# Routing tails, the openings of two phases and where expert weights are fetched, in a two-layer kernel on one core

## The reference

```python
x = x + L0_attn(ln(x))   # a state-space scan: W_in, W_A, W_B, W_C, W_out, rms norm
x = x + L0_ffn(ln(x))    # 8 experts, 2 per token: relu(x @ w1 + b1) @ w2 + b2
x = x + L1_attn(ln(x))   # 16 heads of 16, causal, rotary positions
x = x + L1_ffn(ln(x))    # 16 experts, 2 per token, and a shared expert:
#   shared = silu(x @ Sg) * (x @ Su) @ Sd
#   probs = softmax(x @ Wr); top 2 experts e with weight p:
#   routed = sum of p * (silu(x @ Wg[e]) * (x @ Wu[e]) @ Wd[e])
```

## Time and profile before

| | |
|---|---|
| median of 3 runs | 1963.16 us (1962.06 to 1966.38) |
| the profiled execution | 1963.09 us |
| its span, first to last instruction | 1961.4 us |
| busy TensorE / VectorE / ScalarE / GpSimd | 1638.4 / 1024.0 / 699.0 / 565.0 us |
| instructions | 29495 |

### The profile page before, as it was taken

One profiled execution on the slowest core, in us unless ns is written; L12 is line 12 of the kernel. 1 busy time (PEld: TensorE's weight loads), 2 busy tenths in 40 slices (PEclk: granted clock), 3 DMA queues, 4 the chain that ended last, 5 costly groups with the idle time before them and its releaser, 6 DMA issues. The chain is left out here.

```text
span 1961.4 us, 29495 instructions
## 1 busy us (share of the span) xinstructions
PE 1638.4 (84%) x9849; PEld 1093.9 (56%) x9849; DVE 1024.0 (52%) x2339; ACT 699.0 (36%) x1457; POOL 565.0 (29%) x995
## 2 busy tenths in 40 slices
PE   1999999947999996884799999999999479959910
PEld 0577777644666664442455555555555268848810
DVE  1344445451222223885776666666664258855533
ACT  0444444311222221221065566565556211134400
POOL 2223433350000004883122322222322125510056
PEclk9899999978999997986899999999999789979965
DMA  8001111022222214676645655655552475445444
GB/s 304 20 22 33 49 49 54 33 88 68 64 65 65 65 52 144 217 253 206 94 55 77 103 73 72 96 82 75 94 71 39 130 206 158 146 148 159 151 130 149
DMA packets 151056, 204.05 MB, mean 104 GB/s; under 512 B 20608, under 2 KB 119424, under 8 KB 150656
## 3 DMA queue, kind: packets, MB, share of 16 engines
q1 hardware_dynamic: 104304, 131.12, 30.3%
q10 hardware_dynamic: 34320, 37.50, 5.6%
q0 software_dynamic: 12288, 33.57, 5.4%
HBM read 116.91 MB, written 84.93 MB: 103 GB/s over the span
## 5 line engine op out<-in xcount | busy, mean ns | idle before, releaser
L1690 DVE TENSOR_REDUCE t_row_max<-t_ps_s 128x1 f32<-128x1024 f32 (+7 forms) x512 | 382.0, 757 | 179.8 <-PE t_ps_s L1737 171.9
L1706 ACT ACTIVATE t_probs<-t_ps_st 128x512 f32<-128x512 f32 x576 | 325.6, 596 | 228.9 <-PE t_ps_st L1751 227.2
L1751 PE MATMUL t_ps_st<-t_qs,t_ks 128*128 128x512 f32 (+3 forms) x768 | 277.2, 408 | 0.8 <-ACT t_probs L1706 0.5
L1669 POOL TENSOR_SCALAR_AFFINE_SELECT t_probs<-t_probs 128x128 f32<-128x128 f32 x512 | 139.1, 299 | 395.0 <-ACT t_probs L1706 392.3
L1735 PE MATMUL t_ps_s<-t_ks,t_qs 96*128 96x512 f32 (+3 forms) x768 | 233.5, 358 | 2.2 <-DVE t_row_max L1690 1.9
L1751 PEld LDWEIGHTS t_ps_st<-t_qs,t_ks 128*128 128x128 f32 x768 | 132.0, 192 | 126.5 <-ACT t_probs L1706 100.4
L1767 PE MATMUL t_ps_o<-t_probs,t_vs 128*17 128x256 f32 (+1 forms) x2560 | 185.0, 363 | 0.4 <-issue 0.4
L1349 POOL DMA_INDIRECT d_ye<-outputs_dram,r_pos_all x64 | 64.7, 1011 | 326.1 <-POOLq L1112 308.2
L1735 PEld LDWEIGHTS t_ps_s<-t_ks,t_qs 96*128 96x128 f32 x768 | 136.2, 190 | 21.8 <-DVE t_row_max L1690 15.0
L849 PE MATMUL ps_h<-w_in,xnt 128*128 128x512 f32 x256 | 126.0, 617 | 23.5 <-ACT xnt L683 23.5
L1144 PE MATMUL m_ps_h<-w_sb,m_xt 128*128 x284 | 135.4, 600 | 0.0
(11 more groups left out here) (315 smaller groups left out, 2752.8 us busy)
## 6 DMA issues: line engine op xcount, KB each, us to landing
m_x_t<-gathered_dram SPq DMA_DIRECT2D x150, 128.0 KB, 2.0
outputs_dram<-m_y ACTq DMA_DIRECT2D x150, 128.0 KB, 1.7
t_qs<-qkt_dram SPq DMA_DIRECT2D x128, 128.0 KB, 5.9
t_ks<-qkt_dram SPq DMA_DIRECT2D x128, 128.0 KB, 6.6
qkt_dram<-d_hi SPq DMA_DIRECT2D x32, 256.0 KB, 4.1
qkt_dram<-d_lo SPq DMA_DIRECT2D x32, 256.0 KB, 4.1
headst_dram<-t_att SPq DMA_DIRECT2D x32, 256.0 KB, 7.6
x_t<-in_x_dram SPq DMA_DIRECT2D x8, 512.0 KB, 4.6
```

The source lines that it names most:

```text
L1669: nc.gpsimd.affine_select(out=diag, in_=diag, compare_op=ALU.is_ge, fill=0.0, base=0, pattern=[[1, P]], channel_multiplier=-1).then_inc(ma ...
L1690: nc.vector.reduce_max(row_max[:, p % 2, head * NC + qc:head * NC + qc + 1], ps_s[i % 2][:, 0:(qc + 1) * P], AXX).then_inc(unit_ready, 1)
L1706: nc.scalar.activation(probs[:, p % 2, i // NST, base:base + STC], ps_st[i % 2][:], ACT.Exp, scale=HD ** -0.5).then_inc(exp_ready, 1)
L1751: last = nc.tensor.matmul(ps_st[i % 2][:, col:col + width], ks[:, at, kc * P:(kc + 1) * P], qs[:, at, q0:q0 + width], start=True, stop=True)
```

## The change

- *Lists across partitions* (`front`, `back`): each of the 128 partitions works out one entry of the list (its number is `place_no`), on E elements; two matmuls with the identity turn the two columns `entry` into rows in `ps_list`, and one copy makes `tile_list`.
- *Positions settled in the experts*: the one-hot products that give `pos_all`, and in `back` the end of the softmax, leave the routers; `settle` does them on VectorE at steps 5 to 17 of `run_experts`.
- *Softmax's subtraction* in `back` now stands before the last `place`.
- *Inversions*: three of the four batches' sums are inverted at the end of `attention`; `back` starts with `load(0)` and inverts the last batch behind it.
- *Weights*: the up-weights (two transfers of 2 MB) are fetched by ScalarE at tick 4 of `attention`, the down-weights (2 MB) by ScalarE before `copy_x(2)` of `back`; ScalarE no longer waits there for the shared expert's weights.
- *Scatters* of `back` come a tick later, and the power stands between a group's two halves; `xn` has five buffers instead of four, and the positions are kept for all tiles.
- *Paddings* of `front` read their rows four at a time.
- The shared expert stays in `back` as it was.

The diff, cut to its core. What it does in `front` to the list is the same as in `back`:

```diff
-            for e in range(E):
-                at = sp.value_load(pad_row[0:1, e:e + 1], min_val=e * CAP, max_val=e * CAP + TOK)
-                sp.dma_start(gathered[bass.ds(at, P), :], zeros[:]).then_inc(padded, 16)
+            for e0 in range(0, E, 4):
+                rows = nc.values_load_multi_w_load_instructions(
+                    pad_row[0:1, e0:e0 + 4], engines=[sp.engine], min_val=0, max_val=(E - 1) * CAP + TOK,
+                    skip_runtime_bounds_check_because="a row is a region's start and a count of at most all tokens")[1]
+                for at in rows:
+                    sp.dma_start(gathered[bass.ds(at, P), :], zeros[:]).then_inc(padded, 16)
...
             for i in range(n_list + 3):
+                late(dve, i)
...
+                if tick == pairs:
+                    for s in range(2):
+                        sp.wait_ge(stored[s], 8 * PAIRS * (BATCH - 1))
+                    sp.wait_ge(vs_ready, BATCH)
+                    for b in range(BATCH - 1):
+                        sp.dma_start(sums[:, b, :], sums_of_batch(heads_dram, b)).then_inc(sums_loaded, 16)
+                if tick == pairs + 1:
+                    sp.wait_ge(inv_ready, 1)
+                    for b in range(BATCH - 1):
+                        sp.dma_start(inverse_of_batch(inv_dram, b), sums[:, b, :]).then_inc(inv_stored, 16)
             for s in range(2):
                 sp.wait_ge(stored[s], 16 * (pairs // 2))
+            sp.wait_ge(inv_stored, 16 * (BATCH - 1))
...
+            dve.wait_ge(sums_loaded, 16 * (BATCH - 1))
+            nc.vector.reciprocal(sums, sums).then_inc(inv_ready, 1)
...
+                if tick == 4:
+                    fetch(act)
...
-                if g % 4 == 0:
-                    sp.wait_ge(inv_stored[batch], 16)
+                if g == NG - 4:
+                    sp.wait_ge(inv_stored, 16)
...
-            load_sums(0)
+            load(0)
             for kd in range(KD):
                 sp.dma_start(w_o[:, kd, :], w_o_dram.rearrange("(u e) n -> u e n", e=2 * HD)[:, kd * HD:(kd + 1) * HD, :]).then_inc(w_o_loaded, 16)
-            store_inv(0)
-            for b in range(1, BATCH):
-                load_sums(b)
-            load(0)
             load(1)
...
-            for b in range(1, BATCH):
-                store_inv(b)
+            sp.dma_start(sums[:], sums_of_batch(heads_dram, BATCH - 1)).then_inc(sums_loaded, 16)
+            sp.wait_ge(inv_ready, 1)
+            sp.dma_start(inverse_of_batch(inv_dram, BATCH - 1), inv[:]).then_inc(inv_stored, 16)
             for g in range(2, NG):
                 load(g)
...
-            def scatter(g):
-                pool.wait_ge(pos_ready, g + 1)
-                for j in range(G):
-                    for i in range(2):
-                        nc.gpsimd.indirect_dma_start(
-                            out=gathered[:, :], out_offset=bass.IndirectOffsetOnAxis(ap=pos[:, g % 2, j, i:i + 1], axis=0),
-                            in_=xn[:, g % X, j, :], in_offset=None).then_inc(scattered[g % 2], 16)
-
-            for tick in range(NG + 2):
+            def scatter(g, j):
+                if j == 0:
+                    pool.wait_ge(pos_ready, g + 1)
+                for i in range(2):
+                    nc.gpsimd.indirect_dma_start(
+                        out=gathered[:, :], out_offset=bass.IndirectOffsetOnAxis(ap=pos[:, g * G + j, i:i + 1], axis=0),
+                        in_=xn[:, g % X, j, :], in_offset=None).then_inc(scattered[g % X], 16)
+
+            for tick in range(NG + 3):
+                if live(tick - 3):
+                    scatter(tick - 3, 0)
                 if live(tick):
                     rsqrt(tick)
-                if live(tick - 2):
-                    scatter(tick - 2)
-            for s in range(2):
-                pool.wait_ge(scattered[s], 32 * G * (NG // 2))
+                if live(tick - 3):
+                    scatter(tick - 3, 1)
+            for s in range(X):
+                pool.wait_ge(scattered[s], 32 * G * len(range(s, NG, X)))
...
+            def invert():
+                dve.wait_ge(sums_loaded, 16)
+                nc.vector.reciprocal(inv[:], sums[:]).then_inc(inv_ready, 1)
...
             scale(0)
+            invert()
...
+                if tick == NG + 1:
+                    nc.vector.tensor_tensor(soft[:], logits[:], best[:, :, 0:1].broadcast_to([P, NT, E]), ALU.subtract).then_inc(shifted_ready, 1)
+                    nc.vector.tensor_tensor(soft_best[:], best[:, :, 0:2], best[:, :, 0:1].broadcast_to([P, NT, 2]), ALU.subtract).then_inc(shifted_ready, 1)
...
+            chain.step(nc.vector.tensor_scalar(room[:], n_tiles[:], -float(P), float(CAP), ALU.mult, ALU.add))
             chain.link(nc.vector.tensor_tensor_scan(end[:], one_e[:], n_tiles[:], 0.0, ALU.mult, ALU.add))
-            chain.link(nc.vector.tensor_tensor(passed[:], index[:].unsqueeze(2).broadcast_to([1, n_list, E]),
-                                               end[0:1].unsqueeze(1).broadcast_to([1, n_list, E]), ALU.is_ge))
...
-            nc.vector.tensor_scalar(tile_list[0:1, 0, :], which[:], float(E - 1), None, ALU.min).then_inc(list_ready, 1)
-            nc.vector.tensor_copy(tile_list[0:1, 1, :], first_row[:]).then_inc(list_ready, 1)
-
+            chain.link(nc.vector.tensor_scalar(passed[:, 0], end[:], place_no[:], None, ALU.is_le))
+            chain.link(nc.vector.tensor_tensor(passed[:, 1], passed[:, 0], room[:], ALU.mult))
+            chain.link(nc.vector.reduce_sum(sums_of[:], passed[:], AXX))
+            nc.vector.tensor_scalar(entry[:, 0:1], sums_of[:, 0:1], float(E - 1), None, ALU.min).then_inc(entry_ready, 1)
+            nc.vector.scalar_tensor_tensor(out=entry[:, 1:2], in0=place_no[:], scalar=float(P), in1=sums_of[:, 1:2], op0=ALU.mult,
+                                           op1=ALU.add).then_inc(entry_ready, 1)
             chain.link(nc.vector.tensor_tensor(moved[:], end[:], n_tiles[:], ALU.subtract))
-            chain.link(nc.vector.tensor_scalar(moved[:], moved[:], float(P), None, ALU.mult))
-            chain.link(nc.vector.tensor_tensor(moved[:], moved[:], region[:], ALU.subtract))
-            chain.link(nc.vector.tensor_tensor(hot_all[:], experts[:].unsqueeze(1).broadcast_to([P, 2 * NT, E]),
-                                               best_all[:].rearrange("p t i -> p (t i)").unsqueeze(2).broadcast_to([P, 2 * NT, E]),
-                                               ALU.is_equal))
...
-            chain.link(nc.vector.tensor_tensor(shift[:], shift[:], pos_f_all[:], ALU.add))
-            nc.vector.tensor_copy(pos_all[:], shift[:]).then_inc(list_ready, 1)
-
...
-            dve.wait_ge(exp_ready, 2)
-            soft_chain.link(nc.vector.reduce_sum(soft_sum[:], soft[:], AXX))
-            soft_chain.link(nc.vector.reciprocal(soft_inv[:], soft_sum[:]))
-            nc.vector.tensor_tensor(prob_all[:], soft_best[:], soft_inv[:].unsqueeze(2).broadcast_to([P, NT, 2]), ALU.mult).then_inc(prob_ready, 1)
-            dve.wait_ge(prob_ready, 1)
-            dve.wait_ge(list_ready, 4)
+            chain.link(nc.vector.scalar_tensor_tensor(out=moved[:], in0=moved[:], scalar=float(P), in1=region[:], op0=ALU.mult, op1=ALU.subtract))
+            dve.wait_ge(list_done, 1)
+            nc.vector.tensor_copy(tile_list[:], ps_list[0:1, :, 0:n_list]).then_inc(list_ready, 1)
+            dve.wait_ge(list_ready, 2)
...
-            act.wait_ge(w_loaded, 64)
-            fetch(act)
...
+                if g == 2:
+                    fetch(act)
                 copy_x(g)
                 sigmoid(g)
...
+            pe.wait_ge(entry_ready, 2)
+            for i in range(2):
+                last = nc.tensor.matmul(ps_list[0:1, i, :], entry[:, i:i + 1], ident[:], start=True, stop=True)
+            last.then_inc(list_done, 1)
...
+def settle(dve, nc, kept, i):
+
+
+    steps, E = kept["steps"], kept["E"]
+    here, picks = kept["here"][:], kept["best_at"][:].rearrange("p t i -> p (t i)")
+    if i == 5:
+        steps.at(0)
+        steps.step(nc.vector.tensor_tensor(here, kept["experts"][:].unsqueeze(1).broadcast_to([P, 2 * NT, E]),
+                                           picks.unsqueeze(2).broadcast_to([P, 2 * NT, E]), ALU.is_equal))
+    if i == 7:
+        steps.wait()
+        steps.step(nc.vector.tensor_tensor(here, here, kept["moved"][:].unsqueeze(1).broadcast_to([P, 2 * NT, E]), ALU.mult))
+    if i == 9:
+        steps.wait()
+        steps.step(nc.vector.reduce_sum(kept["shift"][:].rearrange("p t i -> p (t i)"), here, AXX))
+    if i == 11:
+        steps.wait()
+        steps.link(nc.vector.tensor_tensor(kept["shift"][:], kept["shift"][:], kept["pos_f"][:], ALU.add))
+        steps.step(nc.vector.tensor_copy(kept["pos"][:], kept["shift"][:]))
+    if i == 13 and "soft" in kept:
+        steps.step(nc.vector.reduce_sum(kept["sum"][:], kept["soft"][:], AXX))
+    if i == 15 and "soft" in kept:
+        steps.wait()
```

(4 more changed lines are left out.)

196 lines of the change are left out of this document (84 added, 112 removed).

## The result

The changed kernel took 1945.85 us (median of 4 runs, 1941.53 to 1947.91) beside 1962.61 us for the kernel before on the same chip (4 runs, 1961.27 to 1966.38). The ratio is 0.9909, 95% interval 0.9885 to 0.9933: 17 us less, where 15 less (1948.1) had been forecast. The four runs lie in two pairs, 1947.9 twice at a mean granted clock of 0.925 and 1941.5 and 1943.8 at 0.929; the profiled one, 1947.91, is of the slower pair, so its phases together are some 2 us above the median.

A forecast was written before the change was run, and what follows sets the result against it. TensorE bounds the main loops, so gains lie where it stands still, chiefly the opening of `back`. Terms - 18.7 + 7.1 - 3.0 - 1.0 + 0.5 = - 15.1 from 1963.09 give 1948.0, median 1948.1 us; range 1939 to 1957.

The forecast's parts named there:

- 1, opening of `back`: Opening of `back`: without weight issues and three inversions the first group starts earlier, at the upper clock; 18.7 us less.
- The clock's part: Opening of `back`: `go_up(0)` runs at 2.4 GHz instead of 1.2 because TensorE no longer pauses; 1.8 us less.
- The shift: Opening of `back`: with three inversions gone and loads starting sooner, `add_res(0)` starts earlier; 0.8 us less.
- 2, attention: Tick 4 of attention: two up-weight issues on ScalarE delay the exponentials and slow TensorE's clock; 7.1 us more.
- the stall (4.6): Attention: 5.21 us of issues hold the exponentials, two PSUM buffers cover 0.6 us, TensorE waits; 4.6 us more.
- the 2.5 for the clock: Attention: after the idle time TensorE comes back at a lower granted clock; 2.5 us more.
- The rival of nearly free attention: Attention takes the two issues for nearly nothing, 0.7 us, giving 1941.7 us in all; chance 0.14.
- 3 to 5: Down-weights' issue in `back`, three inversions ending attention, power between scatters with five `xn` buffers: each changes nothing.
- 6, list of `back`: End of `back`: VectorE sheds work, scatters get shorter but start 0.8 us later; 3.0 us less.
- 7, list of `front`: End of `front`: the list lies under POOL's scatters, three of which ran long beside it; 1.0 us less.
- 8, positions in the experts: Settling positions on VectorE: nothing in the first experts, slight overrun per tile in the second; 0.5 us more.

The follow-up runs named there:

- e1_weights_only: Kernel before with only the weights moved (up-weights before tick 4 of attention, down-weights before `copy_x(2)` of `back`): 1944.85 us, ratio 0.9906.
- e2_weights_back: Changed kernel with all three weight transfers issued by ScalarE in `back` again, after its wait for the shared expert's weights: 1949.77 us, ratio 0.9930.
- e10_third: Changed kernel with a third 2 MB transfer issued by ScalarE behind the two in attention: 1966.96 us (one run), attention 631.46 us.
- e7_scatter_probe: Changed kernel with three products, three sums and four copies, all unused, added on VectorE behind the list of `front`: first scatter 1.45 us, no kernel time given.
- e3_list_even: Changed kernel with one spare entry in each list row, so the second row starts at byte 320, not 316: 1941.67 us, ratio 0.9893.

## Why the prediction was right, point by point

**1, opening of `back`: right in mechanism and size.** 16.7 us from the start of the phase (16.8 by 16.0 + 0.8), and 2.1 for the clock where 1.8 stood: 18.8 against 18.7. The shift was smaller than forecast (`add_res(0)` at 18.6 us after 19.05, 0.4 less and not 0.8), and the sums landed 0.5 us later than worked out (1561.6; 1556.3 + 4.8 = 1561.1). e1_weights_only shows that the weights alone do it; e2_weights_back shows what the prediction did not see, that without them moved the new order would have been worth 11.3 us instead of 0.8. The clock's part is a matter of luck: 6 of 11 profiles of kernels without the long issue there had the second group 8.4 us behind the first, the others 10.1 to 10.5.

**2, attention: the term was mis-sized.** It stood at 7.1 us; the changed kernel measured 1.6, and from the first pair to the last attention grew by 1.2 to 1.7 in seven profiles. Of its two sizes, the stall (4.6) came from the row of the same two transfers in `back`, 5.21 us. That was the wrong row: the same pair took 5.2 us there, 1.6 in e2_weights_back and 2.3 to 2.8 in attention. That what else is outstanding makes the difference is the reading that fits these rows. TensorE stood still for 1.03 to 1.53 in attention. And the 2.5 for the clock didn't come: after these short pauses the granted clock stayed 1.00, while it was 0.50 after the 3.42 us of the earlier trace rows and 0.67 in the ten us after e10_third's 16.65. The rival of nearly free attention (0.7) was nearer than my term. What sets the second issue's price between 1.1 and 2.4 was not tried.

**3 to 5: right.** The down-weights' issue took 0.38 us and a tick of `back` stays 8.4. The three inversions took 2.55 us on VectorE, 21 us before attention ended, and attention outside its pairs' loop is no longer than before (68.9 us, 69.0 before). `load(2)` was issued at 1563.0 (1557.6 + 4.8 = 1562.4) and cost VectorE 1.18 us at group 2, TensorE none. Scatters grew a little (mean 1048 ns after 998), in time that GpSimd had.

**6, list of `back`: right.** 2.8 us between the second group and the end against 3.0, and 2.9 for the whole phase by e1_weights_only. Both parts show, counted from the last `go_up`: the first of the last four scatters starts 0.7 us later (0.8), and the four take 1.33 us less (1.35). That the two-operand operations were the cause holds, by the finer rule of e7_scatter_probe.

**7, list of `front`: right, and hidden.** From the last positions to the barrier 23.7 us before and 22.7 after: the 1.0 forecast. The phase was 2.4 us longer all the same, for its loop ran at the lower clock for longer. Over all 14 profiles, `front` without the constants took 441.6 to 444.5 us where the granted clock was 0.50 for 52 to 53 us of it (seven profiles), and 446.4 to 447.5 where it was for 62 to 64 (seven). Both kinds occur with either kernel: the kernel before itself took 444.5 and 447.0.

**8, positions in the experts: 0 instead of 0.5.** From tile 4 to tile 19 of `m1_`, over all of `settle`, 25.2 us before and 24.9 after. The 1.5 us of that phase are about 0.5 for the row that begins at byte 316, which I had not seen in the diff, and 1.0 that its tiles 0 to 4 took longer while the clock was still at 0.50. The first experts, put at nothing, took 0.5 us more; the long reads don't explain it (e3_list_even has short ones and the same time), and the cause stays open.

That the total came within 2.3 us thus owes something to chance: 5.5 us too many in attention stood against 3.4 that `front` took more than forecast, 1.0 in `m1_` and 0.8 in the two phases between. Had all four runs been like the faster pair (1941.5 and 1943.8), it would have missed by over 5 us.

## What to carry to other kernels

Take the price of a DMA issue from a queue in the state that the new place will have: here one into an empty queue was 0.44 us, a third 2 MB behind two was 12 to 16, wherever it stood. Spread large transfers over ticks, or give them to the engine with nothing urgent behind. When two parts of a change attack the same wait, measure each with and without the other: here the moved inversions were worth 11 us or nothing. In an opening that waits for transfers, try the order in one queue before a second queue: here the order gained 4.9 us up to the first group and the second queue lost 3.4 of them. And before a difference of 1 or 2 us between two profiles is given to a change, look for it in the stretch that the change touches: `front` and the start of attention vary by more by themselves.

## What was not expected of the hardware

- SyncE's read of four list entries took 0.87 us from a row that begins at byte 316 and 0.30 us from one at byte 320; in the first experts it was the same with 284 and 288.
- A scatter of 0.96 us took up to 1.81 us when the moment 0.13 us after its start fell into a wide VectorE product of two SBUF tensors, and its end then followed that product's by 0.83 us; beside a product it didn't grow when the moment fell into a gap.
- The granted clock rose 6.5 to 9.9 us after the second experts began (6.8 and 9.9 in the same code), and between these the first five tiles differ by 1 us. The phase's time doesn't follow from it alone: two profiles with an early rise (6.8 and 6.9) took 144.3 and 144.4 us, lost in later tiles for no reason that I found.
- The same three weight transfers took 21.0 us to issue, or 13.5 with SyncE's next loads issued behind them instead of before.
